# Reordered reciprocals, limits and copies in a pre-norm attention layer with top-k masking and a gated low-rank layer

## What is computed

```python
qkv = layernorm(x) @ Wqkv.T + bqkv
scores = q @ k.T * SCALE + einsum('bhid,ijd->bhij', q, rel_k[dist])
threshold = top_k(scores, 32)[0][..., -1:]
attn = softmax(where(scores < threshold, -inf, scores))
for i in range(3):
    a_v = attn @ v_curr                      # i == 0: + attn . rel_v[dist]
    v_curr = a_v
    res = res + sigmoid(alphas_raw[i]) * v_curr
x = x + res @ Wout.T + bout
y = layernorm(x)
x = x + y @ base_w.T + base_b + 2 * (y @ lora_A) . lora_B . softmax(y @ router_w.T + router_b)
```

## Time and profile before

| | |
|---|---|
| runs | 703.11, 703.30, 706.62 us; median 703.3 |
| profiled execution | 706.78 us; span of its trace 704.8 us |
| TensorE busy | 654.5 us (93%) |
| VectorE busy | 676.8 us (96%) |
| ScalarE busy | 620.3 us (88%) |
| GpSimd busy | 553.2 us (78%) |
| DMA | 98.7 MB, mean 140 GB/s |
| mean granted TensorE clock | 0.984 of full |

### The profile page before, as it was taken

How to read it: one execution, slowest core, us unless ns; L and a number is a source line. 1 busy time by engine, 2 the same in 40 slices (tenths; PEclk the granted TensorE clock), 3 DMA queues, 4 the chain that set the end, 5 groups by cost and what they waited for, 6 DMA issues and landing times.

```text
span 704.8 us, 20963 instructions
## 1 busy us (share of the span) xinstructions
PE 654.5 (93%) x5780; PEld 510.4 (72%) x5780; DVE 676.8 (96%) x2814; ACT 620.3 (88%) x1772; POOL 553.2 (78%) x985
## 2 busy tenths in 40 slices
PE   4378999999999999999999999999999999999896
PEld 3255777777777777877777777777777777777675
DVE  6899999999999999999999999999999999999973
ACT  3678899999999899999999999998999999998763
POOL 1588898888878888888887888788887888887750
PEclk9779999999999999999999999999999999999998
DMA  6735554544554545454544545454545445454312
GB/s 200 184 117 152 144 155 141 159 137 128 151 156 135 154 136 155 135 154 137 148 141 136 155 137 154 126 164 128 152 135 155 137 128 159 126 154 135 87 58 60
DMA packets 148338, 98.72 MB, mean 140 GB/s; under 512 B 10624, under 2 KB 147968, under 8 KB 148096
## 3 DMA queue, kind: packets, MB, share of 16 engines
q1 hardware_dynamic: 147920, 97.32, 47.4%
q10 hardware_dynamic: 304, 0.08, 0.0%
HBM read 45.59 MB, written 51.77 MB: 138 GB/s over the span
## 4 chain that ended last, share of the span: by engine, by line
DVE 76%; issue 9%; PE 8%; DMA 2%; POOL 2%; ACT 2%; SPq 0%; ACTq 0%; DVEq 0%; POOLq 0%
DVE top L772 39%; DVE work L778 34%; PE ps_p L998 2%; DMA band_scratch<-zeros 1%; PE ps_y L1018 1%; DVE rinv L759 1%; POOL s_sb L330 1%; ACT a_sb L490 1%; PE ps_s L955 1%; PE ps_a L906 1%; PE ps_d L975 1%; PE ps_d L966 0%; DMA band_scratch<-band 0%; PE ps_p L944 0%; DMA skew<-band_scratch 0%
## 5 line engine op out<-in xcount | busy, mean ns | idle before, releaser
L772 DVE MAX8 top<-work 128x8 f32<-128x256 f32 x768 | 284.6, 413 | 0.0
L778 DVE MATCH_REPLACE8 work<-top,work 128x256 f32<-128x256 f32 x512 | 205.9, 410 | 0.0
L330 POOL TENSOR_TENSOR s_sb<-s_sb,pen 128x512 f32<-128x512 f32 x127 | 162.0, 1276 | 39.1 <-ACT pen L480 36.4
L335 POOL TENSOR_SCALAR a_sb<-a_sb,rinv 128x256 f32<-128x256 f32 x254 | 119.3, 481 | 53.1 <-DVE rinv L759 52.3
L490 ACT ACTIVATE a_sb<-s_sb,nmax 128x256 f32<-128x256 f32 x254 | 127.2, 502 | 27.1 <-POOL s_sb L330 19.0
L480 ACT ACTIVATE pen<-s_sb,limit 128x256 f32<-128x256 f32 x254 | 116.3, 510 | 18.7 <-POOL limit L317 18.6
L305 POOL TENSOR_TENSOR s_sb<-s_sb,skew 128x384 f32<-128x384 f32 x128 | 128.5, 1004 | 2.7 <-DMA skew<-band_scratch 2.7
L998 PE MATMUL ps_p<-aT,rows 128*64 128x256 f32 x1024 | 125.0, 385 | 0.4 <-ACT rows L564 0.4
L778 DVE MATCH_REPLACE8 work<-top,s_sb 128x256 f32<-128x256 f32 x256 | 102.9, 410 | 0.0
L772 DVE MAX8 top<-s_sb 128x8 f32<-128x256 f32 x256 | 94.3, 410 | 3.2 <-POOL s_sb L305 3.2
L998 PEld LDWEIGHTS ps_p<-aT,rows 128*64 128x64 f32 x1024 | 67.6, 136 | 38.7 <-issue 10.1
(11 more groups left out here) (169 smaller groups left out, 1313.8 us busy)
## 6 DMA issues: line engine op xcount, KB each, us to landing
skew<-band_scratch SPq DMA_DIRECT2D x128, 192.0 KB, 2.7
diag_scratch<-a_sb SPq DMA_DIRECT2D x128, 192.0 KB, 2.5
band_scratch<-band SPq DMA_DIRECT2D x128, 191.0 KB, 3.5
diag<-diag_scratch SPq DMA_DIRECT2D x128, 128.0 KB, 2.3
wqkv<-in_wqkv SPq DMA_DIRECT2D x1, 1152.0 KB, 8.2
x_sb<-in_x SPq DMA_DIRECT2D x4, 256.0 KB, 5.4
wout<-in_wout SPq DMA_DIRECT2D x1, 512.0 KB, 5.6
out<-xn SPq DMA_DIRECT2D x1, 512.0 KB, 3.2
```

The costliest lines, as they stand in the source:

```text
L330: nc.gpsimd.tensor_tensor(s_sb[g % 4][:], s_sb[g % 4][:], pen[g % 2][:], ALU.subtract).then_inc(pen_added, 1)
L335: nc.gpsimd.tensor_scalar(a_sb[g % 3][:, t, :], a_sb[g % 3][:, t, :], rinv[g % 2][:, t:t + 1], 1.0, ALU.mult, ALU.mult).then_inc(normed, 1)
L772: nc.vector.max(m[:, t, 8 * n:8 * n + 8], src).then_inc(top_step, 1)
L778: nc.vector.match_replace(work[t][:, n % 2, :], m[:, t, 8 * n:8 * n + 8], src, LOW).then_inc(top_step, 1)
```

## The change

It moves steps; it adds one ScalarE instruction, on a 128 x 1 tile.

- VectorE: `divide(g - 1)` goes from behind round 2 of top(g) to its end (but for the last head). The sigmoids go ahead of head 0. `row_moments` goes from behind an odd head to behind the even head after it.
- GpSimd: `normalise(2q - 2)` goes from the end of slot q-1 to behind the first `scale_limit` of slot q; `scale_limit(2q)` goes ahead of `normalise(2q - 1)`; `clip_block`, `scale_wout`, `add_projection` and `second_steps` go further back in the slot.
- ScalarE: in slots 1 and 2 `save_aT` and `save_values` go ahead of the exponentials of the even head. An Exp on the `warm` tile goes ahead of `save_queries(1)`, and the alphas' Exp ahead of `save_queries(2)`.
- SyncE's queue: `load_ffn` goes from behind slot 2 to behind slot 0.

```diff
@@ SyncE
                 slot(q)
                 if q == -1:
                     load_wout()
-                if q == 2:
+                if q == 0:
                     load_ffn()
@@ GpSimd, slot(q)
                 if on(q - 1):
                     scale_limit(2 * q - 1)
-                if on(q - 2):
-                    clip_block(q - 2)
+                    normalise(2 * q - 2)
                 if on(q):
                     negative_max(2 * q)
                 if on(q - 1):
@@
                 if on(q):
                     add_skew(2 * q + 1)
+                if on(q - 2):
+                    clip_block(q - 2)
+                if on(q):
+                    scale_limit(2 * q)
                 if on(q - 1):
                     normalise(2 * q - 1)
                 if on(q):
-                    scale_limit(2 * q)
                     negative_max(2 * q + 1)
-                if 1 <= q <= NP:
-                    scale_wout(q - 1, 0, 2)
-                if q >= NP + 4 and q % NP == 4:
-                    add_projection(q // NP - 1)
-                second_steps(q)
-                if on(q):
                     add_penalty(2 * q)
                 if on(q + 1):
                     add_skew(2 * q + 2)
                 if 1 <= q <= NP:
-                    scale_wout(q - 1, 2, ORDER)
-                if on(q):
-                    normalise(2 * q)
+                    scale_wout(q - 1, 0, ORDER)
+                if q >= NP + 4 and q % NP == 4:
+                    add_projection(q // NP - 1)
+                second_steps(q)
...
@@ ScalarE, slot(q)   (EARLY = 2)
-                if late:
+                copies_first = late or 1 <= q <= EARLY
+                if copies_first:
                     save_aT(2 * q - 1)
                     save_values(q - 1)
                 if on(q):
                     exponent(2 * q)
-                if on(q - 1) and not late:
+                if on(q - 1) and not copies_first:
                     save_aT(2 * q - 1)
                     save_values(q - 1)
@@ ScalarE, ahead of slot 0
-            for q in (-2, -1):
-                save_band(q + 2)
-                if on(q + 1):
-                    save_scores(q + 1)
-                save_queries(q + 3)
+            save_band(0)
+            act.wait_ge(made, MADE)
+            nc.scalar.activation(warm[:, 0:1], warm[:, 0:1], ACT.Exp).then_inc(warmed, 1)
+            save_queries(1)
+            save_band(1)
+            save_scores(0)
             act.wait_ge(late_in, 16 * 8)
             nc.scalar.activation(al[:], al[:], ACT.Exp, scale=-1.0).then_inc(alpha_exp, 1)
+            save_queries(2)
...
@@ VectorE
-                    if n == 2 and g > 0:
+                    if n == (2 if g == HEADS - 1 else ROUNDS - 1) and g > 0:
                         divide(g - 1)
@@
+            dve.wait_ge(alpha_exp, 1)
+            own(nc.vector.tensor_scalar(al[:], al[:], 1.0, None, ALU.add))
+            nc.vector.reciprocal(al[:], al[:]).then_inc(alpha_done, 1)
             for g in range(HEADS):
                 top(g)
-                if g == 0:
-                    dve.wait_ge(alpha_exp, 1)
-                    own(nc.vector.tensor_scalar(al[:], al[:], 1.0, None, ALU.add))
-                    nc.vector.reciprocal(al[:], al[:]).then_inc(alpha_done, 1)
                 q = g // 2
-                if g % 2 == 1 and q >= NP + 4 and q % NP == 4:
+                if g % 2 == 0 and q >= NP + 5 and q % NP == 5:
                     row_moments(q // NP - 1)
```

More of the change, by code:

```diff
@@ L192, in preln_attention_ffn @@
         INSIDE = B - 2
+        EARLY = 2
         DONE = TILES - T
@@ L684, in _ @@
             gate_weights(0, 0, DONE)
+            act.wait_ge(warmed, 1)
             nc.scalar.activation(warm[:, 0:1], warm[:, 0:1], ACT.Sqrt).then_inc(warmed, 1)
@@ L702, in _ @@
             nc.scalar.activation(std[:, DONE:TILES], mv[:, DONE:TILES, 1], ACT.Sqrt, bias=eps[:, 0:1]).then_inc(last_root, 1)
-            act.wait_ge(warmed, 1)
+            act.wait_ge(warmed, 2)
             nc.scalar.activation(warm[:, 0:1], warm[:, 0:1], ACT.Exp).then_inc(warmed, 1)
```

## The result

The changed kernel takes 702.7 us in the median of 22 runs, the kernel before 704.0 in the median of its 22. By the undisturbed runs the ratio is 0.9975 with a 95% interval of 0.9965 to 0.9984: 1.8 us faster, from 1.1 to 2.5. Two of the changed kernel's 22 runs, of 753.13 and 2242.33 us, are disturbed ones and stand outside the ratio. Forecast were 3.5. The direction was right, the size was not.

What follows compares the result with a forecast made beforehand. The prediction took VectorE, busy 96% of the span, as the bound; alphas 0.4, early stalls 2.5 and late stalls 0.6 summed to 3.5 us, taking the median from 703.3 to 699.8 us, range 698.3 to 703.3.

Steps and rivals of the forecast that it cites:

- What bounds, and where the gain must come from: VectorE, busy 96% of the span and 540.00 of 540.00 us from 100 to 640; gain only from the two ends.
- a sign of being wrong: Idle time on VectorE between 100 and 640 us, which the prediction said would show it wrong.
- The reciprocal costs 0.07 us at either place, and the slack grows: VectorE: moving the reciprocal to the head's end changes no cost; slack after the exponentials grows from 0.07 to about 0.7 us.
- The transfers keep their places: SyncE's queue: normalisations some 0.7 us later still find the queue busy, so transfers go out as before; cost nothing.
- rival 3: Late normalisation delays transfers 0.3 us a slot until diagonals push exponentials past the slack: 9.3 us slower, 709.1; chance 0.1.
- The early stalls, 2.5 us: VectorE, 44 to 100 us: all stalls of the six heads concerned gone, 2.5 us; bounds 1.0 to 2.5.
- The part of the loads: `load_ffn` behind slot 2 makes TensorE wait 1.12 us for head 5's diagonals; behind slot 0 they arrive by 63.
- that of the copies: Slot 2: values' copy ahead of the exponentials lets TensorE, which waits 1.61 us, start about 1.3 us sooner.
- The alphas, 0.4 us: VectorE: their two instructions move from between heads 0 and 1 into the 3.2 us wait ahead of head 0; 0.4 us.
- The late stalls, 0.65 of 2.3 us: VectorE, 640 to 670 us: the last wait, 1.4 us, shrinks by 0.65; 0.6 us of it reaches the end.
- the first wait (0.57): VectorE, slots 61 and 62: it stays, as moved `row_moments` no longer delays head 122, eating the 0.65 us gained.
- Rival 1: Median runs lack most early stalls, by another clock phase or faster landings: 2.5 us shrinks to 0 to 1; 702.0; chance 0.2.

Runs made afterwards that it cites:

- after_again: The changed kernel run again unchanged, on another chip: 705.13 us, ratio 0.9993 to the kernel before.
- experiment 2: Both kernels with TensorE transposing a constant tile in place of the fetched diagonals: before 703.34 us, ratio 0.9977; changed 701.56 us, ratio 0.9941.
- start_alone: The kernel before with only the alphas' sigmoids, the warm Exp and ScalarE's copy order ahead of slot 0 changed: 708.23 us, ratio 1.0023.
- experiment 4: The kernel before with only the changed start (708.23 us, ratio 1.0023), its trace compared with others by when the first half clock ended.
- after_again2: The changed kernel run once more unchanged, on the same chip as the experiments' other repeats: 704.87 us, ratio 0.9998 to the kernel before.
- before_no_diag: The kernel before with TensorE transposing a constant tile in place of the fetched diagonals, all transfers still running: 703.34 us, ratio 0.9977.
- before_again: The kernel before run again unchanged: 706.44 us, ratio 0.9997.

## Why the prediction was right and wrong

- **What bounds, and where the gain must come from**: VectorE, at both ends. Right for the one trace, wrong as a statement on the kernel. Other executions of the same program have their waits in the middle as well, and so have the repeats of the changed kernel (heads 87 and 115 in after_again), which the prediction named as a sign of being wrong. I took one execution's stalls for the kernel's.
- **The reciprocal costs 0.07 us at either place, and the slack grows**: right, both in the rows above. The slack grew to 1.0 us and not 0.7, because the exponentials did not keep their places: the limit ends 0.33 us earlier after the selection, and they end 0.28 earlier. (The 0.94 us that the prediction reads between the wait's end and the limit is the normalisation's duration; the rows have 0.90.)
- **"The transfers keep their places"**: the step that failed; its cost stands in the sum as nothing. I took it from one head, 119, whose transfer was issued 0.93 us after its normalisation. In the trace of before the transfers of heads 16 to 117 go out 0.13 us after their normalisations on the mean, and these end 5.5 us after the first MAX8 of the next head; in the changed kernel's trace they end at 6.27 and the transfers go out at 6.50. So the whole lateness, 0.8 us, reached the transfers. The time between the landing of an odd head's diagonals and their use, averaged over the same heads, fell from 2.58 us to 1.12; in the repeats it is 1.81 before and 0.79 and 0.66 after. With that much less cover a slow landing reaches TensorE, then the diagonals' copy, then the exponentials. It is rival 3's mechanism. Its price, by experiment 2, is 0.8 to 2.4 us and not 9.3, but that difference is not clear of the noise. Nor is the order of the steps alone in it: start_alone, in the old order, has a cover of 1.36 us, close to the changed kernel's.
- **The early stalls, 2.5 us**: gone in the one trace, as stated, but this is the term that was too large for the median. The profiled execution of before stood 2.8 us over the median of its 22 runs. In the 14 traces of this study the first MAX8 comes at most 0.6 us earlier than in it, and the stretch from the last MAX8 to the end is at most 0.5 us shorter; what the time holds beside the span (1.7 to 2.0 us) can give 0.3. So, as an estimate from these, 1.4 us or more of its 4.8 us of stalls (2.5 early, 2.3 late) are not in the median execution, and the sum counted 3.1 of them as won there. The part of the loads showed as 2.8 us in one execution, that of the copies as 0.2, and the 1.0 us of heads 4 and 5 hung on the clock too (experiment 4).
- **The alphas, 0.4 us**: seen in the trace (head 0 in 4.99 for 5.41 us); too small to be seen in the times of start_alone.
- **The late stalls, 0.65 of 2.3 us**: in the changed kernel's trace all are gone, in after_again2 head 122 loses 1.7 us behind a wait of 2.0 us for diagonals. The walk through slots 61 and 62 had the first wait (0.57) stay, and in the changed kernel's trace it is gone. The end follows the landings of that execution, and one execution's rows don't give the size.
- **Rival 1** said that the faster runs lack most stalls, by the clock's phase. The first half is the nearest of all to what happened (702.0 from 703.3, 1.3 us of gain, where 1.8 were found). The clock is not excluded as a part of it. It is not the whole: the traces of before and before_no_diag both show TensorE at half clock, 1.2 GHz, from 27 to 44 us, and these executions took 706.8 and 704.2 us. But the 1.0 us of heads 4 and 5 was there only where the half clock lasted that long (experiment 4). And in the 81 executions of before on the three chips, the 28 with a mean granted clock of 0.983 or less have a median of 706.2 us, the 32 with 0.986 or more one of 704.7. Whether the clock makes that difference or goes with the waits that make it, no run separates.

## What to carry to other kernels

Where a step is moved back to give one consumer slack, look at who else reads it: here the normalisation fed a chain of two transfers, whose cover shrank by 1.0 to 1.5 us. Look too at what a later step drags with it: the reciprocal alone at its new place made the kernel slower. Take the cover of a transfer from the mean over all its issues, never from one, and from more than one execution if the runs spread by more than the forecast. And if a queue waits for a landing, put the issues of other transfers into that wait, the urgent one first: moving two calls gave 0.40% on the kernel before, where the whole change gave 0.25% in its first series and 0.02% on the same chip.

## What the runs showed of the hardware

- The same transfer of 192 KB took 2.5 us from issue to landing in the median of one execution of the kernel before and 2.8 in that of another; in three of the changed kernel it took 2.8, 3.2 and 3.1. Most of this lies in what was issued just ahead. From 100 to 640 us of the trace of before, the 17 sends that were issued less than 0.2 us behind another issue have a median of 3.2 us to landing, the 62 issued 1 us or more behind it 2.2. In before_again it is 47 with 3.4 and 41 with 2.2, and in before_no_diag all 106 stand close behind, with 3.4. So an execution of the kernel before has long landings mostly in so far as its queue has fallen behind. In the changed kernel the far ones are slower, 2.6 us in its first trace and in after_again2, and why is open. One of each kind, first from before, then from before_no_diag:

```profile
299.57 0.94 SPq L263 DMA_DIRECT2D band_scratch<-band  x2
301.67 0.36 SPq L237 DMA_DIRECT2D diag_scratch<-a_sb  x1
304.05 0.36 SPq L244 DMA_DIRECT2D diag<-diag_scratch  x1
```

```profile
300.63 0.93 SPq L254 DMA_DIRECT2D skew<-band_scratch  x2
301.65 0.42 SPq L238 DMA_DIRECT2D diag_scratch<-a_sb  x1
306.66 0.36 SPq L245 DMA_DIRECT2D diag<-diag_scratch  x1
```

- A queue that issues as soon as a landing is known can keep itself late: it sends directly behind two other transfers of 190 KB each, lands late, and issues again directly behind the next. In before_no_diag it had 15.1 us to spare, with 364.7 for landings, and in before 106.8 with 277.5; I did not test what tips it from one into the other. In before_no_diag TensorE doesn't wait for the landings, so nothing holds the other engines until the queue has caught up; but start_alone, with that wait and the same order on the queue, had only 54.5 us to spare, with 337.3 for landings.

```profile
SPq L245 <- DMA diag_scratch<-a_sb: 364.7, 128, 4.5
SPq L238 <- POOL a_sb L337: 15.1, 17, 3.1
```
